# Graph attention layers of a fused GNN kernel: the softmax's work on own scores is split off and moved

## The reference, cut to what matters

```python
xw = x @ W                                   # 128 -> 2 heads x 128
xj = xw[src] + edge_emb                      # also one self-loop per node, without edge_emb
alpha = einsum(xw[dst], att_i) + einsum(xj, att_j)      # per edge and head
alpha = leaky_relu(alpha, 0.2)
ea = exp(alpha - segment_max(alpha, dst)[dst])
alpha = ea / (segment_sum(ea, dst)[dst] + 1e-16)
h = segment_sum(xj * alpha[..., None], dst).mean(heads) + b     # relu between layers
```

## Time and profile before

| | |
|---|---|
| median of 3 runs | 5821.73 us (5819.69 to 5822.21) |
| profiled execution, its own time | 5835.43 us |
| its span | 5833.6 us |
| PE busy | 4824.4 us (83%) |
| DVE busy | 4143.7 us (71%) |
| ACT busy | 3247.3 us (56%) |
| POOL busy | 3035.7 us (52%) |
| mean granted TensorE clock | 0.88 of full speed |

### The profile page before, as it was taken

How to read it: one execution, slowest core, us unless ns; L and a number is a source line. 1 busy time by engine, 2 the same in 40 slices (tenths; PEclk the granted TensorE clock), 3 DMA queues, 4 the chain that set the end, 5 groups by cost and what they waited for, 6 DMA issues and landing times. The chain is left out here.

```text
span 5833.6 us, 104695 instructions
## 1 busy us (share of the span) xinstructions
PE 4824.4 (83%) x29899; PEld 4142.3 (71%) x29899; DVE 4143.7 (71%) x15589; ACT 3247.3 (56%) x8537; POOL 3035.7 (52%) x2871
## 2 busy tenths in 40 slices
PE   4999999999959969969969969866995767868666
PEld 3777777777749959959969959844774656746565
DVE  4677777778867668767767768786676667847765
ACT  1777877877736636636636636543772336746500
POOL 0666666655575445445355356222651347555367
PEclk6999999999979979979979979955997778989855
DMA  2999986665545535535535435388663447845332
GB/s 69 167 216 209 210 210 209 210 203 195 192 116 128 123 77 130 117 83 127 111 89 130 104 98 134 87 244 227 151 147 79 138 132 207 233 110 114 66 92 86
DMA packets 1111146, 841.29 MB, mean 144 GB/s; under 512 B 210522, under 2 KB 1063102, under 8 KB 1110256
## 3 DMA queue, kind: packets, MB, share of 16 engines
q1 hardware_dynamic: 1030276, 706.02, 47.0%
q0 software_dynamic: 77040, 128.08, 10.5%
q10 hardware_dynamic: 3264, 0.50, 0.1%
HBM read 390.57 MB, written 448.11 MB: 144 GB/s over the span
## 5 line engine op out<-in xcount | busy, mean ns | idle before, releaser
L747 POOL DMA_INDIRECT gat_G<-table,k_src_row x980 | 1030.8, 1052 | 629.2 <-PE gat_psE L1523 422.5
L1520 PE MATMUL gat_psG<-gat_ends_at,gat_Gw 128*128 128x128 f32 x3920 | 718.5, 279 | 12.3 <-DVE gat_loop L1317 12.3
L1520 PEld LDWEIGHTS gat_psG<-gat_ends_at,gat_Gw 128*128 128x128 f32 x3920 | 599.9, 193 | 15.5 <-issue 12.8
L451 POOL TENSOR_TENSOR nodes_rstd<-nodes_var,k_half 128x14 f32<-128x14 f32 x138 | 360.4, 2612 | 398.1 <-DVE nodes_var L511 390.8
L1521 PE MATMUL gat_psG<-k_ident,gat_loop 128*128 128x128 f32 x1960 | 538.2, 275 | 0.0
L1446 ACT ACTIVATE gat_aggT<-gat_psG 128x512 f32<-128x512 f32 x490 | 292.5, 597 | 396.8 <-PE gat_psE L1523 396.8
L1534 PE MATMUL gat_psZ<-gat_aggT,t_gat_wh 128*128 128x256 f32 x1960 | 504.8, 380 | 1.3 <-ACT gat_hT L1453 1.3
L1523 PE MATMUL gat_psE<-gat_ends_at,gat_wex 128*128 128x128 f32 x1960 | 381.9, 277 | 0.0
L1453 ACT ACTIVATE gat_hT<-gat_psZ,t_gat_bias 128x256 f32<-128x256 f32 x490 | 232.0, 473 | 240.8 <-PE gat_psZ L1535 240.8
L1438 ACT ACTIVATE gat_loop<-gat_own,gat_al 128x128 f32<-128x128 f32 x980 | 335.0, 392 | 49.8 <-DVE gat_al L1291 49.8
L1534 PEld LDWEIGHTS gat_psZ<-gat_aggT,t_gat_wh 128*128 128x128 f32 x1960 | 335.4, 191 | 27.9 <-issue 2.1
(11 more groups left out here) (652 smaller groups left out, 14598.8 us busy)
## 6 DMA issues: line engine op xcount, KB each, us to landing
table<-nodes_rows SPq DMA_DIRECT2D x660, 198.0 KB
table<-nodes_n SPq DMA_DIRECT2D x396, 192.0 KB
gat_own<-table SPq DMA_DIRECT2D x490, 132.0 KB
table<-gat_rows SPq DMA_DIRECT2D x392, 132.0 KB
nodes_x<-in_x SPq DMA_DIRECT2D x132, 192.0 KB
out<-nodes_x_out SPq DMA_DIRECT2D x132, 192.0 KB
gat_ex<-in_ex_pad SPq DMA_DIRECT2D x70, 336.0 KB
gat_G<-table,k_src_row POOLq DMA_INDIRECT x980
```

The lines of the kernel that those rows point to most:

```text
L451: eng.tensor_tensor(rstd[:, k % 3, :], var[:, k % 3, :], K.half[:, 0:M], ALU.pow).then_inc(s.pow, 1)
L747: eng.indirect_dma_start(to, None, table, bass.IndirectOffsetOnAxis(ap=index, axis=0)).then_inc(sem, 16)
L1520: eng.matmul(o[:, h * P:(h + 1) * P], Gw[:, i % RS, t, h, :], ends_at[:, i % RS, t, :], start=True, stop=False)
```

## The change

`scores` on DVE is split in two. `own_scores` takes the lines that need nothing gathered (L1250 or L1252 to L1260, L1262, L1264), with the wait for the masks; `scores` keeps the rest. `own_scores(0)` stands ahead of `source_scores(0)`; in the loop `own_scores(g + 1)` stands at `k` = 2, while `source_scores` stays at `k` = 3 and `scores` at `k` = 4. On PE the three transposes are split as well: `turn_own` does the two of own scores, `turn_scores` the one of gathered scores, which moves from `k` = 1 to `k` = 2 and also waits until `own_scores` is done. `turn_own` stands ahead of everything for group 0, after `aggregate(0)` for group 1 and for the others at the end of the iteration `k` = 6 of the group two before. SP's order, and with it the place where the masks are loaded, is as it was.

```diff
+                def own_scores(g):
                     j = g % 2
                     m = mk[:, j, :, :]
                     c = K.lane_c[:, l:l + 1]
-                    top = stat[:, j, 0, :]
-                    eng.wait_ge(s.scores_turned, g + 1)
+                    eng.wait_ge(s.own_turned, g + 1)
                     eng.wait_ge(mk_in[j], 32 * uses(g, 2))
-                    if g >= 2:
-                        eng.wait_ge(kept, g - 1)
...
                     step(eng.scalar_tensor_tensor(lp[:, 0, :], vb[:, 0, :], c, vb[:, 1, :], ALU.add, ALU.add))
+                    step(eng.scalar_tensor_tensor(lp[:, 0, :], lp[:, 0, :], 0.2, lp[:, 0, :], ALU.mult, ALU.max))
+                    eng.sem_inc(s.own_scored, 1)
+
+                def scores(g):
...
+                    eng.wait_ge(s.scores_turned, g + 1)
+                    if g >= 2:
+                        eng.wait_ge(kept, g - 1)
                     step(eng.scalar_tensor_tensor(e[:, 0, :], psT[0:LN, 0:P], c, vb[:, 1, :], ALU.add, ALU.add))
-                    step(eng.scalar_tensor_tensor(lp[:, 0, :], lp[:, 0, :], 0.2, lp[:, 0, :], ALU.mult, ALU.max))
...
+                own_scores(0)
                 source_scores(0)
                 scores(0)
...
                     if i < NP and g + 1 < NG:
+                        if k == 2:
+                            own_scores(g + 1)
                         if k == 3:
                             source_scores(g + 1)
...
-                def turn_scores(g):
-                    eng.wait_ge(s.sq, g + 1)
+                def turn_own(g):
                     if g >= 1:
-                        eng.wait_ge(s.to_exp, g)
-                    eng.transpose(psT[0:LN, 0:P], sq[:, g % 2, :], K.ident[:, :])
+                        eng.wait_ge(s.al, g)
                     for j in range(2):
                         mm = eng.transpose(psT[0:LN, (j + 1) * P:(j + 2) * P],
                                            K.sc[:, g, 2 * j:2 * j + 2, :].rearrange("p h t -> p (h t)"), K.ident[:, :])
-                    mm.then_inc(s.scores_turned, 1)
+                    mm.then_inc(s.own_turned, 1)
+
+                def turn_scores(g):
+                    eng.wait_ge(s.sq, g + 1)
+                    eng.wait_ge(s.own_scored, g + 1)
+                    eng.transpose(psT[0:LN, 0:P], sq[:, g % 2, :], K.ident[:, :]).then_inc(s.scores_turned, 1)
...
+                turn_own(0)
                 turn_scores(0)
...
-                    if i < NP and g + 1 < NG and k == 1:
+                    if i < NP and g + 1 < NG and k == 2:
                         turn_scores(g + 1)
+                    if i == 0:
+                        turn_own(1)
                     if 1 <= i and i - 1 < NP:
                         mix(i - 1)
...
                     if i < NP and g + 1 < NG and k == 5:
                         turn_weights(g + 1)
+                    if i < NP and g + 2 < NG and k == PG - 1:
+                        turn_own(g + 2)
```

More of the change, by code:

```diff
@@ L1124, in gat_layer @@
         s = A.sems((
-            "seq", "fill_out", "fill_in", "ox_in", "sq", "scores_turned", "step", "to_exp", "exped", "alphas", "alphas_turned", "al",
+            "seq", "fill_out", "fill_in", "ox_in", "sq", "own_turned", "own_scored", "scores_turned", "step", "to_exp", "exped", "alphas", "alphas_turned", "al",
             "weighed", "wex", "loop1", "loop0", "agg", "aggT", "aggE", "mixed", "hT", "rowed", "rows_done", "pieces", "sc", "st_in",
@@ L1237, in source_scores @@
                                       G[:, j, :, D:D + H].rearrange("p t h -> p h t"), K.edge_sc[:, l, g, :, :], ALU.add).then_inc(s.sq, 1)
-                def scores(g):
+                def own_scores(g):
                     j = g % 2
@@ L1262, in scores @@
                     step(eng.scalar_tensor_tensor(lp[:, 0, :], vb[:, 0, :], c, vb[:, 1, :], ALU.add, ALU.add))
+                    step(eng.scalar_tensor_tensor(lp[:, 0, :], lp[:, 0, :], 0.2, lp[:, 0, :], ALU.mult, ALU.max))
+                    eng.sem_inc(s.own_scored, 1)
+                def scores(g):
+                    j = g % 2
+                    m = mk[:, j, :, :]
+                    c = K.lane_c[:, l:l + 1]
+                    top = stat[:, j, 0, :]
+                    eng.wait_ge(s.scores_turned, g + 1)
+                    if g >= 2:
+                        eng.wait_ge(kept, g - 1)
                     step(eng.scalar_tensor_tensor(e[:, 0, :], psT[0:LN, 0:P], c, vb[:, 1, :], ALU.add, ALU.add))
-                    step(eng.scalar_tensor_tensor(lp[:, 0, :], lp[:, 0, :], 0.2, lp[:, 0, :], ALU.mult, ALU.max))
                     step(eng.scalar_tensor_tensor(e[:, 0, :], e[:, 0, :], 0.2, e[:, 0, :], ALU.mult, ALU.max))
```

## The result

The changed kernel takes 5872.3 us (median of 4 runs, 5864.9 to 5880.2) where the kernel before takes 5822.0 (median of 4, 5819.7 to 5824.4): ratio 1.0087, 95% interval 1.0069 to 1.0104. It is slower by 50 us; 5856 was forecast, with a range of 5824 to 5882. Run again beside the experiments it gave 5874.0 (ratio 1.0098, 1.0083 to 1.0114).

What follows compares the result with a forecast made beforehand. PE was taken to bound the loop. From the 5821.7 us median, 14.8 us gained at layer starts and 49.4 us lost to 48 mask-wait stalls gave +34.6 us: 5856 us, range 5824 to 5882.

Steps and rivals of the forecast that it cites:

- What bounds: Layer loop: PE bounds it, busy 346.3 of 350 us; DVE's work costs nothing while DVE keeps ahead.
- The start on DVE: Layer start: own scores run during the gathers' wait, taking 3.96 us off the path in layers 2 to 5, 1.56 in the first.
- the bound: Layer start: masks land by 2118.3, allowing 4.1 us, the slower of the two landings read.
- What is late next at the start: Group 1's gathers, layers 2 to 5: PE waits for them, so some 3.3 of 3.96 us stay; total gain 14.8 us.
- The wait that the move brings: Loop: own scores now wait for masks issued 0.2 us before, stalling PE 1.03 us at the transpose of `sq`.
- The landing: Loop masks: they land 2.85 us after the second issue, between 2.2 and 4.06 us.
- the chain: Loop on DVE: own scores, `one_hot(3)` and copies up to `sq`, 3.58 + 1.55 us, besides `sq` itself and the hand-over.
- How often: Groups 2 to 13 of layers 2 to 5: 48 stalls, 49.4 us in all; none in the first layer.
- The sum: Whole kernel: 49.4 us lost in loops less 14.8 gained at starts, +34.6 us on 5821.7, giving 5856 us.
- The one in which the masks are there in time: Loop rival: masks land within 1.8 us of the second issue, no stall, only the starts' gain, 5807 us; 8%.
- The lower-end one: Loop rival: masks land after 2.2 us, 18 us of stalls against 14.8 gained, 5825 us; 10%.
- Late landing: Loop rival: masks land after 3.6 us or more, stalls of 1.8 to 2.24 us, 5893 to 5914 us; 7%.

Runs made afterwards that it cites:

- e7: Changed kernel with own_scores(g + 1) behind source_scores at k = 3, except group 0's call, which stays at k = 2: 5811.3 us, ratio 0.9983.
- e3: Changed kernel with own_scores(0) behind source_scores(0) at a layer's start, loop left as changed: 5877.5 us, ratio 1.0096.
- e1: Changed kernel with SP issuing load_group(g + 2) at k = 4 instead of load_group(g + 1) at k = 0, so masks load earlier: 5806.2 us, ratio 0.9969.
- e5: Changed kernel with the edge-feature DMA (336 KB) issued ahead of the two mask DMAs in load_group: 5984.6 us, ratio 1.0284.
- e4: Changed kernel keeping only the start; in the loop the order of the kernel before, own_scores(g + 1) directly ahead of scores(g + 1) at k = 4: 5829.8 us, ratio 1.0012.
- e8: Kernel before the change, with only SP's load_group(g + 2) issued at k = 4 so masks load earlier: 5824.4 us, ratio 1.0004.

## Why the prediction was right, point by point

- *What bounds.* Right: PE bounds the loop, DVE's work costs nothing by itself. e7 shows the strongest form of it.
- *The start on DVE.* Right: 1.93 us to 0.69 in the first layer and 4.33 to 0.69 later were the forecast; L1271 follows `sq` by 0.69 us. The masks came sooner than the bound reckoned: own scores started 2.3 us after the second mask issue (DVE had waited 5.82 us for them), 9 us before `sq`.
- *What is late next at the start.* Right in kind for layers 2 to 5: PE waits 1.20 us for group 1's gathers in the second layer (0.88, 0.45 and 0.45 in the others), and 3.3, 3.8, 3.5 and 3.9 us stay, against 3.3 forecast. Wrong in size for the first layer: 1.56 forecast, 3.5 measured. There DVE had waited longer for group 1's gathers, 4.62 us against 2.01 in the second layer, and PE with it at `k` = 1, and the move to `k` = 2 took most of that wait away (0.63 us are left; e3 keeps 3.2 of the 3.5 us with the move alone). I had worked out only the own scores' share. Sum 18.0 against 14.8. The first layer of the kernel before:

```profile
1717.11 0.20 DVE L1236 TENSOR_TENSOR gat_sq<-gat_G,t_edge_sc 128x28 f32<-128x28 f32 x1 [4.62 <-DMA gat_G<-table,k_src_row]
...
1717.37 0.28 PE L1492 MATMUL gat_psT<-k_ident,gat_sq 128*28 128x128 f32 x1 [3.28 <-DVE gat_sq L1236]
```

- *The wait that the move brings.* Right, and shown by taking it away (e1), by enlarging it (e5) and by having less behind it (e7). The landing, which no row gave, was taken as 2.85 us after the second issue; own scores started 3.05 us after it on average (2.06 to 4.37 over 48 groups). The trace of the kernel before held the landing all the same: there the last rise of the masks' semaphore comes 2.97 us after the second issue on average, from 1.99 to 4.38. The chain from the own scores to `sq` took 5.20 us against 5.13.
- *How often.* Right: PE waited in all 48 groups of layers 2 to 5 and in none of the first (its rest is 375.8 against 375.6 us).
- *The sum.* The total was too low, 34.6 us against 50.3, and most of that is in the loop: 65.5 us where 49.4 were forecast. The stall itself was nearly right. Measured as the forecast has it, as the delay of the transpose of `sq` behind the matmul before it, it is 1.16 us per group (1.27 against 0.11 before), 55.7 in all, against 1.03. The landing makes 9.6 us of the difference (0.20 x 48) and the chain 3.4; a hand-over from `sq` to PE of 0.27 us instead of 0.33 gives back 2.9, and PE coming to the transpose 0.08 us later than reckoned 3.8. Two terms stood at nothing in the sum. The clock, which I had left at full, costs 3.4 us in the loops: of the 48 stalls only the two longest, 2.46 and 2.16 us, were followed by a dip. After the latter the stretch from 2215 to 2220 us has a granted clock of 0.66, 1.7 us lost. And e1 shows 4.0 us more than before with no stall at all. Together that is 63.1 of the 65.5 us; the remaining 2.4 are less than what two executions of this kernel differ by.

```profile
2215.00:2220.00 5.00, 5.00 (x25) 4.59 (x26) 4.79 (x18) 1.44 (x4) 0.26 (x1) 0.66 0.15 38
```

- *The rivals.* The one in which the masks are there in time fell: DVE never started on them within 1.8 us of the second issue. The lower-end one fell too. It was near the estimate of 2.1 us that I worked out from the Trainium skill (DMA: Bandwidth & Descriptors, Anatomy of one DMA). The Trainium skill fits that figure to GpSimd's path, while these loads are SP's; that it is meant for a quiet machine was my own addition, which it does not state. The shortest distance seen here, 2.06 us, is near it; the mean is 1 us more. Late landing, 3.6 us or more, happened in 13 of the 48 groups (up to 4.37 us), not on average.

## What to carry to other kernels

When a step is moved ahead, list every wait inside it and look up when each is fulfilled in the old trace: here the compute itself fitted at its new place, and the load issued 0.2 us before its new use cost 60.7 and 65.5 us in two executions. A landing that nobody waits for is not in the list of waits, but the trace's semaphore records have it. If the ring allows it, move the load's issue with the step (e1: 50 us slower became 17 us faster). A gain at a start lasts only as far as the next thing that is pinned elsewhere; e4 gave back more than it had won.

## What the runs showed of the hardware that was not expected

Short stalls of PE are not harmless to its clock. Stalls of 3.4 and 4.39 us were followed by stretches at a mean granted clock of 0.54 and 0.59, and even one of 2.16 us by 0.66, where those of 2.10 us and less in the same execution left it at 1.00. In e5, with stalls of 2.48 us on average, 29 of 48 were followed by such a dip, and this made a delay of 1.5 us per group cost 2.4 us. The length of the stall alone does not settle it: in e5 one of 1.89 us was followed by a dip and one of 2.70 us was not. At the start of the first layer the stall of 3.28 us shown above left the clock at 1.00, and one of 2.59 us in e8, at the same place of the same order on PE, halved it; what decides is not shown. The first line is the kernel before, the second and third are e8:

```profile
1717.30:1720.70 3.40, 3.33 (x25) 3.15 (x26) 3.23 (x13) 1.05 (x3) 2.49 (x3) 1.00 0.26 60
...
1717.19 0.39 PE L1492 MATMUL gat_psT<-k_ident,gat_sq 128*28 128x128 f32 x1 [2.59 <-DVE gat_sq L1236]
...
1717.10:1720.10 3.00, 2.91 (x9) 2.33 (x10) 2.86 (x12) 0.00 (x0) 2.39 (x3) 0.50 0.26 68
```

Small mask loads (49 KB each) released DVE 2.06 to 4.37 us after the second issue, from group to group, in one execution of one program.
